# Joining pairs of the softmax denominators' sums on VectorE before TensorE multiplies them

## The reference

```python
q, k = rope(q), rope(k)                      # 32 heads of 32, keys repeated for 4 query heads
scores = einsum('bhqd,bhkd->bhqk', q, k) / sqrt(32)
scores = where(causal, scores, -1e20)
attn = softmax(scores, axis=-1)              # exp(s - max) / sum(exp(s - max))
out = einsum('bhqk,bhkd->bhqd', attn, v)
```

## Time and profile before

| | us |
|---|---|
| median of 3 runs | 3659.36 |
| profiled execution, whole | 3663.12 |
| its span, first to last instruction | 3661.3 |
| PE busy | 3428.2 (94%) |
| DVE busy | 2269.7 (62%) |
| ACT busy | 1413.6 (39%) |
| POOL busy | 2237.4 (61%) |

### The profile page before, as it was taken

One profiled execution on the slowest core, in us unless ns is written; L12 is line 12 of the kernel. 1 busy time (PEld: TensorE's weight loads), 2 busy tenths in 40 slices (PEclk: granted clock), 3 DMA queues, 4 the chain that ended last, 5 costly groups with the idle time before them and its releaser, 6 DMA issues. The chain is left out here.

```text
span 3661.3 us, 63504 instructions
## 1 busy us (share of the span) xinstructions
PE 3428.2 (94%) x25088; PEld 2380.1 (65%) x25088; DVE 2269.7 (62%) x3912; ACT 1413.6 (39%) x1660; POOL 2237.4 (61%) x1037
## 2 busy tenths in 40 slices
PE   2988888989999999999999999999997699999999
PEld 1777777855666666666666666666663278888887
DVE  3665666667777777777677777777771444444443
ACT  2222222214555555555555555555555200010010
POOL 5322222018899889989998998999898022222222
PEclk9999999979999999999999999999999699999999
DMA  8887777341221222122112212211210634443432
GB/s 247 209 197 199 195 189 195 93 91 35 58 54 38 56 54 51 39 61 52 41 47 58 50 39 60 54 49 39 63 31 9 215 69 93 91 94 94 92 92 63
DMA packets 249954, 325.52 MB, mean 89 GB/s; under 512 B 64090, under 2 KB 157914, under 8 KB 249730
## 3 DMA queue, kind: packets, MB, share of 16 engines
q1 hardware_dynamic: 231298, 255.29, 26.8%
q0 software_dynamic: 18432, 67.12, 8.3%
HBM read 223.74 MB, written 97.52 MB: 88 GB/s over the span
## 5 line engine op out<-in xcount | busy, mean ns | idle before, releaser
L721 DVE TENSOR_REDUCE mpart<-mx_ps 128x1 f32<-128x512 f32 (+3 forms) x2560 | 1432.6, 605 | 520.0 <-PE mx_ps L774 339.1
L690 ACT ACTIVATE probs<-st_ps 128x1024 f32<-128x1024 f32 (+1 forms) x1152 | 1063.6, 974 | 854.4 <-PE st_ps L805 623.4
L771 PE MATMUL mx_ps<-k_max,qs 96*128 96x512 f32 (+3 forms) x2560 | 908.6, 417 | 18.0 <-POOL masks L639 15.1
L805 PE MATMUL st_ps<-qs,k_score 98*128 98x512 f32 (+1 forms) x2304 | 723.7, 409 | 0.2
L664 POOL TENSOR_TENSOR sums<-probs 128x1024 f32<-128x1024 f32 x256 | 609.6, 2381 | 160.8 <-ACT probs L690 160.7
L771 PEld LDWEIGHTS mx_ps<-k_max,qs 96*128 96x128 f32 x2560 | 467.9, 195 | 295.3 <-DVE mpart L721 188.6
L666 POOL TENSOR_TENSOR sums<-sums,probs 128x1024 f32<-128x1024 f32 x256 | 608.6, 2377 | 26.0 <-ACT probs L690 7.3
L823 PE MATMUL od_ps<-probs,vs 128*32 128x256 f32 (+1 forms) x9216 | 592.8, 375 | 0.0
L672 POOL TENSOR_TENSOR sums<-sums,probs 128x1024 f32<-128x1024 f32 (+1 forms) x256 | 538.7, 2104 | 20.4 <-ACT probs L690 0.4
L805 PEld LDWEIGHTS st_ps<-qs,k_score 98*128 98x128 f32 x2304 | 422.0, 194 | 72.9 <-ACT probs L690 11.9
L1037 POOL TENSOR_TENSOR h<-h,bb 128x1024 f32<-128x1024 f32 x32 | 105.1, 3285 | 542.7 <-DVE xn_c L1135 542.7
(11 more groups left out here) (105 smaller groups left out, 4014.4 us busy)
## 6 DMA issues: line engine op xcount, KB each, us to landing
qs<-q_hi_scratch SPq DMA_DIRECT2D x128, 256.0 KB, 4.5
h_scratch<-hbuf SPq DMA_DIRECT2D x32, 512.0 KB, 3.5
q_hi_scratch<-rot_hi SPq DMA_DIRECT2D x64, 256.0 KB
q_lo_scratch<-rot_lo SPq DMA_DIRECT2D x64, 256.0 KB
qs<-q_lo_scratch SPq DMA_DIRECT2D x64, 256.0 KB, 5.6
o_scratch<-od_sb SPq DMA_DIRECT2D x128, 128.0 KB
o_in<-o_scratch SPq DMA_DIRECT2D x32, 512.0 KB, 4.4
o_in<-recip_scratch SPq DMA_DIRECT2D x128, 128.0 KB, 7.8
```

The costliest lines, as they stand in the source:

```text
L690: nc.scalar.activation(probs[:, n % SLOTS, half, :, lo:QW], st_ps[:, half, :, lo:QW], ACT.Exp, scale=float(HD) ** -0.5).then_inc(exp_done, 1)
L721: nc.vector.tensor_reduce(mpart[:, h * TPC + t, kc:kc + 1], mx_ps[:, e % MAX_BANKS, 0:w], AX, ALU.max).then_inc(max_done, 1)
L771: mm = nc.tensor.matmul(out, qs[c][0:K_ROWS, h, t * P:(t + 1) * P], k_max[0:K_ROWS, kc * CT:kc * CT + w], start=True, stop=not diagonal)
L805: mm = nc.tensor.matmul(out[:, :, lo:QW], k_score[0:M_ROW + 2, kt * P:(kt + 1) * P], qs[c // 2][0:M_ROW + 2, h:h + 2, at + lo:at + QW], st ...
```

## The change

Where a chunk of queries has two or more full sets (two steps each), VectorE adds the sums of pairs of them, the later into itself, and TensorE multiplies the joined sum once. The pairs are sets 4 and 5, 7 and 8, 10 and 11, 14 and 15, 16 and 17, 18 and 19, so 6 of the 20 sets of denominator products a group are left out, 96 in all. A join of a set that ends at step s stands in VectorE's list ahead of the entries of step s+2 (`JOIN_LAG`), behind a wait for POOL's `sum_done`. TensorE's denominators of a joined set wait for `joined` in place of `sum_done`. POOL may write again in the slot of the earlier set of a pair only when the joined set has been multiplied (`USED_BY`).

```diff
--- before.py
+++ after.py
@@ -448,6 +448,24 @@
 
 SETS = sum_sets()
 SET_OF = [j for j, steps in enumerate(SETS) for s in steps]
+JOIN_LAG = 2
+
+
+def joined_sets():
+
+
+    joined = {}
+    for c in range(QH):
+        whole = [j for j, steps in enumerate(SETS) if STEPS[steps[0]][0] == c and len(steps) == 2]
+        while len(whole) >= 2:
+            joined[whole[-1]] = whole[-2]
+            whole = whole[:-2]
+    return joined
+
+
+JOINED = joined_sets()
+JOINS = sorted(JOINED)
+USED_BY = [next((k for k in JOINS if JOINED[k] == j), j) for j in range(len(SETS))]
 LEAD, FIRST_LEAD = 18, 12
 TURN_AFTER = 5
 
@@ -513,7 +531,8 @@
         max_ready, max_done, max_all = sem("max_ready"), sem("max_done"), sem("max_all")
         m_hi_done, m_rows = sem("m_hi_done"), sem("m_rows")
         st_ready, exp_done = sem("st_ready"), sem("exp_done")
-        sum_step, sum_done, batch_done = sem("sum_step"), sem("sum_done"), sem("batch_done")
+        sum_step, sum_done, joined = sem("sum_step"), sem("sum_done"), sem("joined")
+        batch_done = sem("batch_done")
         od_copied = sem("od_copied")
         stored = [sem(f"stored{s}") for s in range(2)]
         LOAD, STORE = 3 * 16, 2 * 16
@@ -654,7 +673,7 @@
                 wide = [(s, k) for s in SETS[j] for k in range(2) if k == 0 or s not in diagonal]
                 if q >= SUM_SLOTS:
                     g_old, j_old = divmod(q - SUM_SLOTS, len(SETS))
-                    pool.wait_ge(batch_done, g_old * NS + SETS[j_old][-1] + 1)
+                    pool.wait_ge(batch_done, g_old * NS + SETS[USED_BY[j_old]][-1] + 1)
                 if len(wide) == 1:
                     exp_waited(g, diagonal[0], 1)
                     nc.gpsimd.tensor_tensor(at[:, :, P:QW], probs_of(g, diagonal[0], 0, P),
@@ -745,13 +764,28 @@
 
             def group(g, first, last):
                 for s in range(NS):
+                    join(g, s - JOIN_LAG)
                     for more, n in entries_in(s, first, last):
                         take(g + more, n)
+
+            def join(g, s):
+
+                if s < 0:
+                    g, s = g - 1, s + NS
+                j = SET_OF[s]
+                if g < 0 or j not in JOINED or s != SETS[j][-1]:
+                    return
+                q = g * len(SETS) + j
+                into, other = (sums[:, (q + k) % SUM_SLOTS] for k in (0, JOINED[j] - j))
+                dve.wait_ge(sum_done, q + 1)
+                nc.vector.tensor_tensor(into, into, other, ALU.add).then_inc(joined, 1)
 
             for k in range(FIRST_LEAD):
                 for n in AT_STEP[k]:
                     take(0, n)
             groups(group)
+            for s in range(NS - JOIN_LAG, NS):
+                join(GROUPS - 1, s)
 
         @block.tensor
         def _(pe):
@@ -831,7 +865,10 @@
                 n, j = g * NS + s, SET_OF[s]
                 q = g * len(SETS) + j
                 lo = P if SETS[j] == (s,) else 0
-                pe.wait_ge(sum_done, q + 1)
+                if j in JOINED:
+                    pe.wait_ge(joined, g * len(JOINS) + JOINS.index(j) + 1)
+                else:
+                    pe.wait_ge(sum_done, q + 1)
                 if lo:
                     for h in range(GROUP):
                         nc.tensor.matmul(od_ps[h * HD:(h + 1) * HD, 1, 0:lo], ones[:], probs[:, n % SLOTS, 0, h, 0:lo],
@@ -843,7 +880,7 @@
 
             def products(g, s):
                 mm = values(g, s)
-                if s == SETS[SET_OF[s]][-1]:
+                if s == SETS[SET_OF[s]][-1] and SET_OF[s] == USED_BY[SET_OF[s]]:
                     mm = denominators(g, s)
                 mm.then_inc(batch_done, 1)
```

## The result

The changed kernel takes 3972.63 us (median of 4 runs, 3972.08 to 3973.97), the kernel before 3660.77 us beside it. The ratio is 1.0853, with a 95% interval of 1.0839 to 1.0866: 312 us slower. The forecast was 4009 us, its range 3800 to 4060 us. The profiled execution has a span of 3972.2 us.

What follows compares the result with a forecast made beforehand. TensorE's gapless stream bounds the attention stage, POOL the last group. Sets 5 and 8 add 94 us, sets 11, 15, 17 and 19 251, with the tail 350, giving 4009 us as median; range 3800 to 4060.

Steps and rivals of the forecast that it cites:

- What bounds: Attention stage: TensorE's instruction stream is the path, so a microsecond added there lengthens the result; POOL bounds the last group.
- Part 1, the gain is absorbed: TensorE's 96 removed denominator products: booked as a gain of 0, though estimated at 40 us if nothing stops.
- it only arrives earlier at the same stop: Step ahead of each join: time saved by the left-out product only lengthens TensorE's wait, gain 0.
- Part 2, the place of the stops: Joins hold up VectorE's reductions, stopping TensorE at a step's fourth maxima entry, e3: 4.0 us for set 5.
- The port's share: Joins of 5, 11, 17 wait for POOL's running addition at the shared SBUF port: 1.28, 1.28, 2.38 us.
- Sets 11 and 17: Joins in steps 22 and 33: TensorE stops of 4.7 and 5.1 us, each plus 2.5 us of clock.
- Part 3, the clock: Behind large stops TensorE runs at half clock, costing 1.7 us for set 5, 2.5 each for 11 and 17.
- Part 4: Other moved waits: TensorE's wait for `joined` and POOL's wait for the sums' slots each cost 0.
- the tail: Last group, where POOL is the path: three joins stop it and the last stands in the path, 5 us.
- The cover: Rival: VectorE's idle covers the joins and the products are simply saved, 3619 us; chance 0.07.
- No port conflict: Rival: joins don't wait for POOL's additions, stops are shorter and too short for the clock, 3808 us; chance 0.1.
- Clock up: Rival: the port conflict holds but TensorE's clock doesn't fall behind the stops, 3907 us; chance 0.15.

Runs made afterwards that it cites:

- e2_products_out: Kernel before with the denominator products of the six joined sets left out and no joins: 3620.72 us.
- e1_products_back: Changed kernel with each join written to a tile of its own and all twenty products back: 4016.5 us.
- e6_pool_waits: Changed kernel with POOL starting the set behind a joined one only when the join is done: 3921.78 us.
- e9_only_17: Changed kernel with only the join of set 17 with 16 left, its one product saved: 3765.01 us.
- e5_filled: Changed kernel with TensorE multiplying zeros ahead of its stop in the steps of joins 5, 11, 17 and 19: 3876.22 us.
- e10_small: Changed kernel with only the joins of sets 8 and 15 left: 3679.96 us.
- e7_step_later: Changed kernel with joins three steps behind their set, products four, and six slots for the sums: 3791.04 us.
- e4_one_input: Changed kernel with each join replaced by a reduction of one whole SBUF tile behind the same wait: 3902.12 us.
- e3_wait_only: Changed kernel with each join cut to a reduction of eight columns behind the same wait: 3829.14 us.
- e12_dma_joins: Changed kernel with joins made by POOL-issued accumulating DMAs instead of VectorE, products four steps behind, six slots: 3672.02 us.

## Why the prediction was right, and where it was off

- *What bounds.* Right: TensorE without a gap; e2_products_out shows that 0.44 us out of its stream are 0.44 us off the period.
- *Part 1, the gain is absorbed.* Partly wrong. The step that failed is "it only arrives earlier at the same stop", which took the end of a stop as fixed. It is fixed for the joins of 5, 8, 15 and 19; for 11 and 17 POOL's sum comes earlier, with the scores and their exponentials. With the clock held up the six products are worth 15 us, not 0. In the change as it stands they are worth 44 us (e1_products_back), close to the full price, of which 29 come by way of the clock; the prediction had no term for that either.
- *Part 2, the place of the stops.* Right: VectorE waits for POOL, then for the port, and TensorE stops at entry e3. The port's share was set at 1.28, 1.28 and 2.38 us; measured are 1.05, 1.05 and 2.14 beyond 1.22, since a blocked join ends 1.08 us after POOL's addition, not 1.22. The pair in the earlier trace rows said so already: L1112 ends 1.09 us after L1037, which the prediction read as one join-length. The Trainium skill's rule ("SBUF — State Buffer", "Who interferes with whom") is borne out by these durations, and e6_pool_waits shows it from the other side.
- *Sets 11 and 17.* Their stops were set at 4.7 and 5.1 us and measured 4.07 and 3.78. The term that was mis-sized is POOL's end: I took it from the rows of before, relative to a TensorE that hadn't stopped yet. I had seen the effect for sets 8, 15 and 19 and left it out here. e9_only_17 confirms it for set 17: alone, the join of 17 waits 2.35 us as in the rows of before.
- *Part 3, the clock.* Right that it falls behind the large stops; the share is shown by e5_filled. It was set at 1.7, 2.5 and 2.5 us and measured 1.56, 1.74 and 1.57. Missed: the fall behind the 1.11 us stop of set 19, another 1.58. The sum, 6.7, came out near the 6.5 measured by a cancellation, which was luck.
- *Part 4 and the tail.* No wait for `joined` in the periods: all four waits of the denominators for a join in the profile stand in the last group. The fourteen periods between the second group's start and the last's give 14 x 20.6 = 288 us of the 311; the first group grew by 10.4, and everything from the last group's first score product to the end by 12.9 us, of which the joins of 19, 5 and 8 are 8.7 and the tail with the rest 4.2, against 5 forecast.
- *The rivals.* The cover doesn't hold where the sum is late (e10_small) or POOL's addition is in the way (sets 11, 15 and 17 in e7_step_later); it does hold in e7_step_later for the joins of 19, 5 and 8 taken together, which cost less than their products save. No port conflict: what that would give is e4_one_input, 3902 us, not the 3808 I had, because its stops still lower the clock. (In that rival the stop of set 17 is 2.3 + 0.4, as its sum has it, not the 2.4 + 0.4 written; and the sum of the forecast gives a period of 148.8, not 148.) Clock up: 3876 measured by e5_filled, 3907 forecast.

The 20.6 us of a period, then: the wait for the sums leaves 5.7 us of idle (e3_wait_only), the join's length 2.5 more (e4_one_input), the port 5.2 more (after), the clock costs 6.9 (e5_filled), and the products' 2.6 us come off. That is 17.7. The other 2.9 us make no gap. They stand in the joins' own steps, where the shift with the saved product is 0.2 to 0.9 us longer than TensorE's gap; how they come about there isn't shown, and I take them for entries that follow each other more slowly behind the stop. The clock's 6.9 us don't stand beside the three other causes: the stops bring the falls, and those of the wait alone already bring most of them (19.0 of 20.5 us a period at 1.2 GHz in the profiled execution of e3_wait_only, whose faster runs had a granted clock of 0.938 and 0.939 over the kernel against its 0.931).

## What to carry to other kernels

An engine with 27% idle is not free for a 1.2 us instruction if the engine that bounds the kernel is only three buffers away from it: look for the last moment at which the inserted instruction may end, and set it against the time when its input is ready. Price an addition of two SBUF tiles on VectorE by what GpSimd is doing at that moment, and price a stop of TensorE by its length and by the slower clock behind it. When several stops are inserted, follow the producers' state through the first before pricing the next. And judge such insertions one by one: with a sum that was ready and POOL idle or just ending its addition, a join of 1.2 us cost TensorE 0.2 to 0.5 us, about what its product saves or less (sets 19 and 5 of e7_step_later).

## What the runs showed of the hardware

- A VectorE addition of two 128x1024 f32 SBUF tiles, 1.22 us alone, took 2.27 us when POOL had begun an addition of 1.26 us 0.07 us earlier, and 3.36 us when POOL's was of 2.35 us. POOL's following addition took 3.22 in place of 2.38 us. A reduction of one SBUF tile at the same place took 1.22 us always.
- POOL's next addition starts some 0.04 us before the last one's end, VectorE answers a semaphore 0.03 us after it. At each of the four joins a period behind which POOL had an addition ready, the waiting VectorE lost the port to it.
- TensorE's clock fell to 0.50 for 3.4 us behind a stop of only 1.11 us, in all fourteen periods. In e12_dma_joins it stayed at 1.00 behind one of 1.18 us, so these stops' length alone doesn't tell. Keeping the array at products of zeros in the stops kept the clock at 1.00 and made the kernel 97 us faster.
- An accumulating DMA of 128x1024 f32 from SBUF to SBUF, issued by POOL, took 0.86 us of POOL and 4.9 us (median) to landing.
